# Mamba scan stage: ScalarE's step-size chain placed over states 5 to 10 of an item, VectorE's block for it at state 10, GpSimd's hold at state 12

## The reference, cut to what matters

```python
xz = einsum('bld,ed->ble', x, wi); xin, z = split(xz, 2)
u = silu(cb + causal_conv(xin, cw))
xdbl = einsum('blc,ec->ble', u, xpw)       # dt_in (32), Bc (16), Cc (16)
dt = softplus(einsum('blr,cr->blc', dt_in, dw) + db)
A = -exp(Alog)
# scan over tokens, 16 states per channel, 256 channels
dA = exp(dt_t[..., None] * A)
h = dA * h + (dt_t * u_t)[..., None] * B_t[:, None, :]
y = einsum('bcn,bn->bc', h, C_t)
# then
y = (y + u * Dp) * silu(z)
m = layernorm(x + einsum('blc,dc->bld', y, wo)) * g + b
```

## Time and profile before

| | |
|---|---|
| time, median of 3 runs | 2210.42 us (2202.44 to 2212.16) |
| the profiled execution's own time | 2202.75 us |
| its span in the profile | 2200.9 us |
| PE busy | 1873.3 us (85%) |
| DVE busy | 1626.5 us (74%) |
| ACT busy | 1327.4 us (60%) |
| POOL busy | 1013.3 us (46%) |

### The profile page before, as it was taken

How to read it: one execution, slowest core, us unless ns; L and a number is a source line. 1 busy time by engine, 2 the same in 40 slices (tenths; PEclk the granted TensorE clock), 3 DMA queues, 4 the chain that set the end, 5 groups by cost and what they waited for, 6 DMA issues and landing times. The chain is left out here.

```text
span 2200.9 us, 49437 instructions
## 1 busy us (share of the span) xinstructions
PE 1873.3 (85%) x19547; PEld 1375.3 (62%) x19547; DVE 1626.5 (74%) x2594; ACT 1327.4 (60%) x2696; POOL 1013.3 (46%) x778
## 2 busy tenths in 40 slices
PE   7888888888888678987877777798688699999999
PEld 4444444444443335445667777767676599999999
DVE  3999999999999994867653332336544588998897
ACT  5777787778877643133533334252346488888886
POOL 1777777777777780100046666400350033333333
PEclk9999999999999998997889889899798699999999
DMA  3444444444444432600057777501640321121100
GB/s 128 160 133 130 124 147 134 129 129 127 138 137 141 140 111 54 136 8 7 21 178 214 214 217 219 151 10 41 222 145 15 145 88 52 66 74 61 33 6 7
DMA packets 98037, 241.63 MB, mean 110 GB/s; under 512 B 15024, under 2 KB 48320, under 8 KB 95504
## 3 DMA queue, kind: packets, MB, share of 16 engines
q1 hardware_dynamic: 89120, 218.12, 32.5%
q0 software_dynamic: 7680, 15.74, 2.8%
q10 hardware_dynamic: 1008, 4.62, 0.6%
HBM read 226.25 MB, written 12.19 MB: 108 GB/s over the span
## 5 line engine op out<-in xcount | busy, mean ns | idle before, releaser
L1126 POOL TENSOR_TENSOR dBu<-du,Bs 128x858 f32<-128x858 f32 (+1 forms) x240 | 589.7, 2459 | 198.2 <-DVE hst L1053 109.4
L576 PE MATMUL py<-hst,ident 128*128 128x429 f32 (+1 forms) x960 | 402.1, 546 | 82.2 <-DVE hst L1063 81.6
L1053 DVE TENSOR_TENSOR_SCAN hst<-dA,dBu 128x858 f32<-128x858 f32 (+1 forms) x240 | 457.7, 1907 | 12.3 <-ACT dA L894 9.2
L894 ACT ACTIVATE dA<-dt,negA 128x416 f32<-128x416 f32 (+1 forms) x480 | 269.6, 596 | 147.6 <-DVE hst L1053 146.7
L576 PEld LDWEIGHTS py<-hst,ident 128*128 128x128 f32 x960 | 178.5, 197 | 271.1 <-DVE hst L1063 153.1
L3451 POOL TENSOR_TENSOR hm<-h,mw 128x264 f32<-128x264 f32 x128 | 90.0, 703 | 390.6 <-DVE h L3431 390.6
L1063 DVE TENSOR_TENSOR hst<-hst,Cs 128x858 f32<-128x858 f32 (+1 forms) x240 | 247.1, 1030 | 0.0
L3322 PE MATMUL pg<-hs,wh 128*128 128x66 f16 x6144 | 218.0, 193 | 6.6 <-issue 6.3
L3322 PE MATMUL pg<-xm,wi 128*128 128x66 f16 x6144 | 216.1, 195 | 4.2 <-issue 2.9
L2848 ACT ACTIVATE eh<-ph,wb 128x128 f32<-128x128 f32 x384 | 108.9, 371 | 172.5 <-PE ph L2721 115.6
L3322 PEld LDWEIGHTS pg<-hs,wh 128*128 128x128 f16 x6144 | 203.9, 98 | 10.6 <-issue 7.2
(11 more groups left out here) (567 smaller groups left out, 3417.2 us busy)
## 6 DMA issues: line engine op xcount, KB each, us to landing
wb<-sf_w SPq DMA_DIRECT2D x96, 514.0 KB
Bs<-bc_rows SPq DMA_DIRECT2D x96, 429.0 KB, 4.6
Cs<-bc_rows SPq DMA_DIRECT2D x96, 429.0 KB, 3.5
mw<-route_weights SPq DMA_DIRECT2D x8, 2112.0 KB, 10.1
wb<-gf_w SPq DMA_DIRECT2D x24, 514.0 KB
Bs<-bc_rows SPq DMA_DIRECT2D x24, 396.0 KB, 5.2
Cs<-bc_rows SPq DMA_DIRECT2D x24, 396.0 KB, 4.6
mb<-route_masks SPq DMA_DIRECT2D x8, 1088.0 KB, 12.6
```

The source lines that it names most:

```text
L576: return nc.tensor.matmul(out, weight, moving, **kw)
L894: last = a(o, by_seq(dt[:, j % 2, h, 0:n])[:, :, 1:S], ACT.Exp, scale=negA[:, l, h * DST + k:h * DST + k + 1])
L1053: v.tensor_tensor_scan(hst[:, g % HR, 0:2 * n], dA[:, g % 2, 0:2 * n], dBu[:, g % 2, 0:2 * n], 0.0, ALU.mult, ALU.add).then_inc(h_ready, 1)
L1126: g_.tensor_tensor(dBu[:, g % 2, 0:2 * n].rearrange("p (a n) -> p a n", a=2), du[:, j % 2, :, 0:n], Bs[:, q % NBS, k % BG, 0:n].unsqueeze( ...
```

## The change

ScalarE's step-size activations are placed at other states. `delta` keeps `mag` and `pos` at 3 and 4, and does the first Exp (e) and the Relu (low) at 5. `steps` does the Exp and Square of low at 8, the two Ln at 9 and the last Exp at 10. Before, e stood at 4, Relu, Exp and Square at 5, the two Ln at 7, the last Exp at 8. `logs` now stands ahead of `steps`. On VectorE, `soften` moves from state 8 to state 10; `back` stays at 8. On GpSimd, the hold for `m` stays at 10 and the hold for `du` moves to 12. No instruction is added or taken away.

```diff
--- before.py
+++ after.py
@@ -809,24 +809,24 @@
                         act.wait_ge(dt_done, j)
                     a(mag[:, h, 0:n], bank(j, f"d{h}")[:, 0:n], ACT.Abs).then_inc(mag_ready, 1)
                     a(pos[:, h, 0:n], bank(j, f"d{h}")[:, 0:n], ACT.Relu).then_inc(d_read, 1)
-                if k == 4:
+                if k == 5:
                     act.wait_ge(mag_ready, 2 * j + 2)
                     a(e[:, :, 0:n], mag[:, :, 0:n], ACT.Exp, scale=-1.0).then_inc(e_ready, 1)
-                if k == 5:
                     a(low[:, :, 0:n], mag[:, :, 0:n], ACT.Relu, scale=-1.0, bias=edge[:, 4:5]).then_inc(capped, 1)
+
+            def steps(j, k):
+                l, at, n = item(j)
+                if k == 8:
                     act.wait_ge(capped, j + 1)
                     a(low[:, :, 0:n], low[:, :, 0:n], ACT.Exp, scale=-1.0, bias=edge[:, 4:5]).then_inc(w_ready, 1)
                     act.wait_ge(w_ready, j + 1)
                     a(low[:, :, 0:n], low[:, :, 0:n], ACT.Square, scale=KAPPA, bias=edge[:, 1:2]).then_inc(sq_w_ready, 1)
-
-            def steps(j, k):
-                l, at, n = item(j)
-                if k == 7:
+                if k == 9:
                     act.wait_ge(sq_w_ready, j + 1)
                     a(low[:, :, 0:n], low[:, :, 0:n], ACT.Ln, bias=edge[:, 2:3]).then_inc(low_logged, 1)
                     act.wait_ge(e_ready, j + 1)
                     a(e[:, :, 0:n], e[:, :, 0:n], ACT.Ln, bias=edge[:, 0:1]).then_inc(ln_ready, 1)
-                if k == 8:
+                if k == 10:
                     act.wait_ge(low_logged, j + 1)
                     a(low[:, :, 0:n], low[:, :, 0:n], ACT.Exp, scale=-0.5, bias=edge[:, 3:4]).then_inc(low_ready, 1)
 
@@ -908,7 +908,7 @@
             project(0, 14)
             for k in (3, 4, 5):
                 delta(0, k)
-            for k in (7, 8):
+            for k in (8, 9, 10):
                 steps(0, k)
             act.wait_ge(l_loaded, 112)
             a(whh[:, :, :, :], whh[:, :, :, :], ACT.Copy, scale=0.5).then_inc(lw_ready, 1)
@@ -951,10 +951,10 @@
                     project(j + 2, k)
                 if k == 7 and j < LSTM_ITEMS:
                     nc.scalar.preload_act_table_set("natural_log_exp_and_others")
-                if k in (7, 8) and j + 1 < NI:
-                    steps(j + 1, k)
                 if k == 7 and j >= 2:
                     logs(j - 2)
+                if k in (8, 9, 10) and j + 1 < NI:
+                    steps(j + 1, k)
                 if k == 9 and j < LSTM_ITEMS:
                     nc.scalar.preload_act_table_set("exp_and_others")
                 if j == NI - 1 and k == 10:
@@ -1076,11 +1076,10 @@
                         lstm_h(PER_ITEM * j + (k - 2) // 4)
                 if j >= 1 and k == 1:
                     gate(j - 1)
-                if k == 8:
-                    if j + 1 < NI:
-                        soften(j + 1)
-                    if j >= 2:
-                        back(j - 2)
+                if k == 8 and j >= 2:
+                    back(j - 2)
+                if k == 10 and j + 1 < NI:
+                    soften(j + 1)
                 if k == 15 and j >= LAST + 2:
                     fuse(j - LAST - 2)
             weigh(NI * DST - 1)
@@ -1114,11 +1113,10 @@
                 q = g // BG
                 if k == 0:
                     pool.wait_ge(du_done, j + 1)
-                if k == 10:
-                    if j + 1 < NI:
-                        pool.wait_ge(du_done, j + 2)
-                    if j >= 2:
-                        pool.wait_ge(m_scaled, j - 1)
+                if k == 10 and j >= 2:
+                    pool.wait_ge(m_scaled, j - 1)
+                if k == 12 and j + 1 < NI:
+                    pool.wait_ge(du_done, j + 2)
                 if g % BG == 0:
                     pool.wait_ge(b_loaded[q % NBS], 16 * (q // NBS + 1))
                 if g >= 2:
```

## The result

The changed kernel takes 2229.99 us, the median of 4 runs (2224.68 to 2231.17), against 2206.78 us for the kernel before (4 runs, 2202.44 to 2212.16). The ratio is 1.011, with a 95% interval of 1.0088 to 1.0131: slower by 1.1%. The profiled execution took 2224.68 us, with a span of 2222.8; against that of before, which took 2202.75, it is 21.9 us more, where the prediction's sum was 15.

What follows compares the result with a forecast made beforehand. VectorE's queue was taken to bound the Mamba stage. The walk's 14.0 us plus 1.3 in weighs gave 15 us more: 2218 from the profiled execution, 2225 from the median, taken as 2221 us, range 2200 to 2233.

Steps and rivals of the forecast that it cites:

- The old waits of state 5 go: VectorE at state 5: waits for the LSTM gates vanish, 2.2 us in item 7 with dA's, all 15.0 us of gates.
- ScalarE then waits for x0 and x1: ScalarE, now earlier, waits for TensorE's x0 and x1 before its copies u0 and u1: 0.85 and 0.94 us in item 7.
- rival 2: TensorE's x0 and x1 come earlier than the rows say, so ScalarE doesn't wait: -7 us, 2196 to 2203; chance 0.12.
- Scan 9 waits for dA, 1.4 us in item 7: VectorE before scan 9: dA(9) lands late, 1.4 us of new waiting in item 7, 0.2 to 2.4 in LSTM items.
- The walk: Step-by-step timing of ScalarE's and VectorE's queues in each item through scan 12, summing to 14.0 us lost.
- The gates of state 9 cost 2.1 us an item and 3.3 in the first two: VectorE at state 9 waits for ScalarE's gates: eleven waits near 2 us, 3 in items 0 and 1.
- The wait at scan 12 goes: VectorE's wait for dA(12), 0.2 us in item 7 before, vanishes because soften now comes ahead of scan 11.
- `soften` after the hold costs 1.3 us in weighs: Second GpSimd multiply begins inside the weigh before scan 12: 0.24 us in 5 or 6 items, 1.3 us in all.
- rival 5: More than +20 us: SBUF port price of 21 us on top, 2239, or late z0 or lagging y adds; chance 0.1.
- rival 1: ScalarE's turns at states 8 to 10 are as walked: +10 to +18 us, 2213 to 2229; chance 0.5.

Runs made afterwards that it cites:

- the swap at state 8: Kernel before with Exp and Square of low moved from state 5 to state 6, behind the gates: 2153.58 us, ratio 1.0001.
- The spread version: Changed kernel with Exp, Square at 7, Ln at 8 and 9, last Exp and soften at 9, du hold 11, constants 13: 2135.54 us, 0.9926 to kernel before.
- The short Ln: Changed kernel with both Ln cut to 8 of 858 columns, step size then wrong: 2158.16 us, ratio 1.0026 to the kernel before.

## Why the prediction was right in its direction and short in its size

- *The old waits of state 5 go:* right, 15.0 became 0.8 us. That there was little to gain by clearing them alone was shown by the swap at state 8, 12.4 us for 15.0. The spread version clears them and gains, so they are not a price that every order pays.
- *ScalarE then waits for x0 and x1:* right. ScalarE waits for `side` at L781 16 times, up to 2.0 us, 15.3 in all. The modelled ends of the matmuls held, and rival 2 fell.
- *Scan 9 waits for dA, 1.4 us in item 7:* too high. Seven items wait, 6.8 us in all, and item 7 not at all. The walk took the times of d, x0 and x1 from the profile of before ("the change doesn't speed it up"). In item 7 x1's matmul ended 12.98 us after scan 4 there (450.54 - 437.56), and 11.30 after it in the changed kernel (464.19 - 452.89). Behind that stands TensorE's clock at state 2. In the profile of before it fell there in items 0 to 3 and 6 to 8, and in all of these but item 0 `mag` waited about 2.1 us for TensorE. In the changed kernel it fell in items 1 and 6, and a little in item 0. Item 7 before (TensorE's timeline, then the busy time over six us):

```profile
431.97 2.93 PE L576 MATMUL py<-u,diag 128*128 128x429 f32 x4 [1.69 <-DVE yz L1011]
```

```profile
431.97:437.97 6.00, 6.00 (x12) 3.11 (x13) 6.00 (x6) 2.10 (x6) 3.73 (x3) 0.72 0.33 116
```

  The same stretch of item 7 in the changed kernel, and `mag` there, which now waits 0.5 us and not 2.2:

```profile
447.30:453.30 6.00, 6.00 (x28) 3.32 (x30) 6.00 (x6) 4.02 (x10) 3.56 (x2) 1.00 0.35 98
```

```profile
451.21 0.53 ACT L810 ACTIVATE mag<-side 128x429 f32<-128x429 f32 x1 [0.48 <-PE side L576]
```

  From scan 4 to scan 12 the walk's 14.0 us measured 6.9. In items 2, 3, 7 and 8, where the clock fell before and didn't after, it had put 4.0 us of loss and there were 2.2 of gain. Item 0 was put at 3.3 and lost 1.6. In every other LSTM item it was right within 0.25 us. It isn't the lag at state 1 that comes back here: in the run with the projection moved there is no such lag in front of item 7, and scan 9 waits the same 6.8 us. Why the clock fell at state 2 in one profile and not in the other stays open.
- *The gates of state 9 cost 2.1 us an item and 3.3 in the first two:* right, 24.9 us in eleven waits. The short Ln took 15 us off them.
- *The wait at scan 12 goes:* right, none is left.
- *`soften` after the hold costs 1.3 us in weighs:* not there. All weighs together took 247.1 us before and 246.7 after. For what the hold guards against, 0.24 us was the wrong price: 1.4 us was measured; it did not bear on the time since the hold stayed.
- *The step that failed:* the walk ended at scan 12 and took the rest of the item as unchanged; TensorE's lag stood only in rival 5, as "y adds that lag", with the reason that it had been seen late against `hst` once. It costs 9.5 us at state 1 and 4.2 at the fused sums of items 12 and 13, 13.7 us. I asked what stood ahead of `soften` in VectorE's queue and not what stood behind it, and I took TensorE's times as fixed. With `soften` at state 10 TensorE idles up to 4.6 us in one piece, right in front of the rest of the item, and its clock falls behind that in eight of items 0 to 9. What shows it: with `soften` moved alone the waits are there, with one projection taken out from behind the add they are nearly gone, and in no profile of the changed kernel is an item whose clock stayed at 1.00 followed by one.

The sum of 15 against 21.9 is then: 13.7 missing at state 1 and the fused sums, 1.3 too many for the weighs, and 7.1 too many in the walk from scan 4 to scan 12; the remaining 1.6 is rounding, the start of the first item (0.4 us) and the parts of states 1 to 4 that no `ig` wait holds. By the prediction's own list this is rival 5, more than +20, which had a chance of 0.1, and not rival 1, +10 to +18, which had 0.5. That the time still lies in the range (2230 in 2200 to 2233) is in part luck: two errors of opposite sign, 13.7 and 7.1 us, and for the most part both come from TensorE's clock, of which the prediction says nothing.

## What to carry to other kernels

When a block of work moves to a later place in one engine's queue, list what now stands behind it, and which engine idles for that with ready work in its own queue; that engine's lag comes out an item later. If that engine is TensorE, look at the granted clock behind the idle time, before and after: a copy of its times from the profile of before holds only where the clock stays as it was. When one engine feeds another through an in-order queue, add up what stands ahead of each handover and hold it against the consumer's time until it comes for it: here that arithmetic led from a losing placement to one that beat both, with the same instructions. And a wait that vanishes from the list of waits isn't gained until the next handover of the same engine has been looked at.

## What the runs showed of the hardware that was not expected

A VectorE operation on two SBUF operands that meets a running GpSimd multiply takes 2.42 us instead of 1.04, and ends 0.91 us after the multiply; its length in the profile is then mostly waiting, though the profile counts it as busy.

TensorE's granted clock can fall for a few us behind a single idle stretch inside a stage whose mean is 0.94: 0.56 over the 2.93 us after 4.43 us of idle time, with four matmuls at 2.94 us instead of 1.71, and 0.72 over six us in the kernel before after 1.69 us of idle time. It isn't the same in every item or every profile of one kernel (0.55 behind item 3 and 1.00 behind item 5 of one execution), so that part of such a loss changes from run to run.
